# Block 1 of a gated linear attention kernel: four rows of Q times state move from VectorE to GpSimd, and the engines' calls are put in other orders

## The reference

```
state = state * f[i] + v[i] * k[j]        # 8x8 per head, scan over 1024 tokens
o[i]  = sum over j of state[i, j] * q[j]
```

## Time and profile before

| | |
|---|---|
| median of 3 runs | 510.62 us (509.84 to 511.73) |
| the profiled execution | 511.23 us |
| its span, first to last instruction | 509.4 us |
| mean granted TensorE clock | 0.998 of full speed |
| busy TensorE (products) | 495.7 us |
| busy VectorE / ScalarE / GpSimd | 447.6 / 404.9 / 311.0 us |
| moved by DMA | 87.33 MB |

### The profile page before, as it was taken

How to read it: one execution, slowest core, us unless ns; L and a number is a source line. 1 busy time by engine, 2 the same in 40 slices (tenths; PEclk the granted TensorE clock), 3 DMA queues, 4 the chain that set the end, 5 groups by cost and what they waited for, 6 DMA issues and landing times. The chain is left out here.

```text
span 509.4 us, 7961 instructions
## 1 busy us (share of the span) xinstructions
PE 495.7 (97%) x2528; PEld 383.1 (75%) x2528; DVE 447.6 (88%) x708; ACT 404.9 (79%) x839; POOL 311.0 (61%) x362
## 2 busy tenths in 40 slices
PE   9989999999999999999999999999999999999995
PEld 5667787777877777777877777777877777777895
DVE  3999999999989999999899999899999899992352
ACT  5765878787888977888897887889878788868764
POOL 0742839577592838768384775848385784929341
PEclk9999999999999999999999999999999999999999
DMA  7997999935797779768988895905875850700001
GB/s 244 250 269 181 258 257 226 234 87 150 186 264 195 221 178 239 187 164 201 248 210 214 209 257 150 244 2 145 209 181 154 218 126 18 190 1 1 23 2 65
DMA packets 21772, 87.33 MB, mean 171 GB/s; under 512 B 2528, under 2 KB 3552, under 8 KB 13792
## 3 DMA queue, kind: packets, MB, share of 16 engines
q1 hardware_dynamic: 21440, 86.46, 66.9%
q10 hardware_dynamic: 288, 0.33, 0.2%
HBM read 74.72 MB, written 12.06 MB: 170 GB/s over the span
## 5 line engine op out<-in xcount | busy, mean ns | idle before, releaser
L915 ACT ACTIVATE h<-F,cols 128x512 f32<-128x512 f32 x120 | 80.4, 688 | 11.3 <-PE F L2345 10.6
L489 POOL TENSOR_TENSOR h1lo<-h,h1hi 128x512 fp32r<-128x512 f32 x60 | 76.2, 1289 | 11.9 <-ACT h1hi L908 11.8
L489 POOL TENSOR_TENSOR h2lo<-h,h2hi 128x512 fp32r<-128x512 f32 x60 | 76.0, 1288 | 6.7 <-ACT h2hi L908 6.6
L1601 DVE TENSOR_TENSOR_SCAN KJ<-g,carry,KJ 128x512 f32<-128x512 f32 x64 | 78.2, 1262 | 0.0
L2345 PE MATMUL F<-h2hi,whi 128*128 128x512 f32 (+1 forms) x256 | 74.7, 424 | 0.2
L1601 DVE TENSOR_TENSOR_SCAN KJ<-g,KJ 128x512 f32<-128x512 f32 x64 | 74.3, 1203 | 0.7 <-POOL KJ L537 0.4
L1608 DVE TENSOR_TENSOR QJ<-QJ,KJ 128x1024 f32<-128x1024 f32 x60 | 71.2, 1213 | 0.2
L2345 PE MATMUL F<-h1hi,whi 128*128 128x512 f32 (+1 forms) x256 | 68.9, 411 | 2.4 <-DVE h L1665 2.1
L550 POOL TENSOR_TENSOR KJ<-KJ,v_sb 128x512 f32<-128x512 f32 x32 | 42.4, 1332 | 43.9 <-DMA KJ<-qk_bounce 26.9
L2345 PE MATMUL F<-h1lo,whi 128*128 128x512 f32 (+1 forms) x256 | 67.1, 401 | 0.0
L2345 PE MATMUL F<-h2lo,whi 128*128 128x512 f32 (+1 forms) x256 | 65.8, 398 | 0.4 <-POOL h2lo L489 0.3
(11 more groups left out here) (183 smaller groups left out, 934.9 us busy)
## 6 DMA issues: line engine op xcount, KB each, us to landing
KJ<-qk_bounce SPq DMA_DIRECT2D x30, 1024.0 KB, 9.9
QJ<-qk_bounce SPq DMA_DIRECT2D x30, 1024.0 KB, 10.7
qk_bounce<-qk SPq DMA_DIRECT2D x30, 256.0 KB, 4.0
x_in<-in_x SPq DMA_DIRECT2D x16, 256.0 KB, 9.1
xT<-in_xT SPq DMA_DIRECT2D x15, 256.0 KB, 4.9
out<-res SPq DMA_DIRECT2D x15, 256.0 KB, 5.8
wraw<-in_wffn SPq DMA_DIRECT2D x2, 1024.0 KB, 9.4
wraw<-in_wffn SPq DMA_DIRECT2D x2, 256.0 KB, 4.7
```

Source lines behind the costliest of these rows:

```text
L489: e.tensor_tensor(h_lo[layer][:, t, :w], h[:, t, :w], h_hi[layer][:, t, :w].bitcast(f32), ALU.subtract).then_inc(lo_done[layer], 1)
L915: e.activation(dst[:, t, :WIDTH[n]], F[t][:, :WIDTH[n]], ACT.Gelu, scale=scale[t]).then_inc(gelu_done[layer], 1)
L1601: e.tensor_tensor_scan(K, g[:, :WIDTH[n]], K, init, ALU.mult, ALU.add).then_inc(scan_done, 1)
```

## The change

1. In block 1, GpSimd multiplies rows 0 to 3 of QJ by the states, in four calls of 128x512 (the new function qs_gp). VectorE keeps rows 4 to 7 (qs(1,2), qs(1,3)). Who waits for QJ of block 1 (sum_transposed(1), the fetch of K of block 3) waits for both counts.
2. kv_gp and qs_gp take the DMA's half by the row; the counting functions are written with two tables, KV_FIRST and QS_FIRST. For kv nothing changes by it.
3. save_carry waits for the one before it.
4. The lists of calls of all five engines and the table FREED are in another order. The calls themselves are the same ones. Quoted are block 0 and 1 and the places that the prediction speaks of; several hundred further lines move by one to some places.

```diff
@@ tables and counts
+    KV_FIRST, QS_FIRST = {1: 2}, {1: 2}
+        def kv_first(n):
+            return KV_FIRST.get(n, 3)
+        def qs_first(n):
+            return QS_FIRST.get(n, 0)
+        def qs_pairs(n):
+            return sum(NPAIR - qs_first(m) for m in range(1, n))
+        def qs_gpsimd(n):
+            return sum(2 * qs_first(m) for m in range(1, n))
@@ sync, fetch
-                        e.wait_ge(qs_done, NPAIR * (n - 2))
+                        e.wait_ge(qs_done, qs_pairs(n - 1))
+                        e.wait_ge(qs_gp_done, qs_gpsimd(n - 1))
@@ gpsimd
+            def qs_gp(n, j):
+                if j % 2 == 0:
+                    e.wait_ge(Q_landed[2 * j // HD][n % 2], fetched(n))
+                e.wait_ge(scan_done, HD * n + j + 1)
+                Q = rows(QJ, n)[:, j, :]
+                e.tensor_tensor(Q, Q, rows(KJ, n)[:, j, :], ALU.mult).then_inc(qs_gp_done, 1)
@@ scalar, save_carry
+                if n:
+                    e.wait_ge(carry_done, n)
@@ vector, add
-                e.wait_ge(qs_done, NPAIR * (n - 1) + p + 2)
+                e.wait_ge(qs_done, qs_pairs(n) + p + 2)
@@ tensor, sum_transposed
-                    e.wait_ge(qs_done, NPAIR * n)
+                    e.wait_ge(qs_done, qs_pairs(n + 1))
+                    e.wait_ge(qs_gp_done, qs_gpsimd(n + 1))
@@ gpsimd, order of blocks 0 and 1
             qsj_gp(0)
             kvj_gp(2)
             kvj_gp(4)
+            qsj_gp(1)
+            qsj_gp(2)
             scale_w3()
-            qsj_gp(1)
             kvj_gp(6)
-            qsj_gp(2)
             qsj_gp(3)
             kv_gp(1, 4)
             rstd_of(0, "o")
             kv_gp(1, 5)
             kv_gp(1, 6)
             rstd_of(0, "1")
+            qs_gp(1, 0)
+            qs_gp(1, 1)
             kv_gp(1, 7)
+            qs_gp(1, 2)
+            qs_gp(1, 3)
             lo(1, 0, 0)
@@ vector, order of blocks 0 and 1
+            scan(0, 4)
             kvj(7)
-            scan(0, 4)
+            qsj(4)
             scan(0, 5)
-            qsj(4)
+            qsj(5)
             scan(0, 6)
-            qsj(5)
+            qsj(6)
             scan(0, 7)
-            qsj(6)
+            qsj(7)
             kv(1, 0)
-            qsj(7)
+            stats_o(0)
             kv(1, 1)
-            stats_o(0)
             scan(1, 0)
+            half_norm("o")
             scan(1, 1)
-            half_norm("o")
+            gated_y0()
             scan(1, 2)
-            gated_y0()
-            scan(1, 3)
             residual_1(0)
             find_low_parts()
             stats_1(0)
+            scan(1, 3)
             scan(1, 4)
+            half_norm("1")
             scan(1, 5)
             scan(1, 6)
             set_flag()
-            half_norm("1")
-            qs(1, 0)
-            qs(1, 1)
             x1_lo(0)
             scan(1, 7)
-            qs(1, 2)
             hmul(0, 0)
             hmul(0, 1)
+            qs(1, 2)
             qs(1, 3)
@@ scalar, the new order from the end of block 0's attention
+            tanh(3)
+            silu_gate(0)
+            norm_o(0)
+            silu_gate(1)
+            affine(0)
+            split_weights(1)
+            sum_low_parts(3)
+            copy_k(3)
+            center_w3()
+            norm_1(0)
+            copy_q(2)
+            split_weights(2)
+            x1_hi(0)
+            split_weights(3)
+            silu(0, 0)
+            silu(0, 1)
+            copy_v(2)
+            silu_gate(2)
@@ scalar, block 5's q (before: copy_v(5), hi(2, 2, 3), copy_q(5))
             gelu(1, 2, 3)
+            copy_q(5)
+            norm_2(1)
             hi(2, 2, 3)
@@ tensor, before the loop
-            project_gate(0)
             sum_j(6)
             sum_j(7)
+            project_f(3)
             keep_busy(4, back)
+            keep_busy(1, back)
+            project_gate(0)
             project_gate(1)
+            transpose_y(0)
             project_v(2)
-            keep_busy(1, back)
-            project_f(3)
-            transpose_y(0)
             project_k(3)
             attention_out(0)
             keep_busy(10, F[3])
-            count_low_parts()
             project_q(2)
             keep_busy(16, F[3])
             transpose_x1(0)
+            count_low_parts()
@@ tensor, start of the loop
-                project_q(3)
                 up_hi(0, 2, low_parts)
-                up_lo(0, 2, low_parts)
                 up_hi(0, 3, low_parts)
+                up_lo(0, 2, low_parts)
                 up_lo(0, 3, low_parts)
+                project_q(3)
                 sum_transposed(1)
@@ tensor, blocks 13 and 14
-                project_gate(15)
                 mid_hi(2, 13, 1, low_parts)
...
                 up_lo(14, 3, low_parts)
+                project_gate(15)
                 mid_open(1, 14, 0, low_parts)
@@ vector, blocks 14 and 15
+            kv(15, 0)
             stats_o(14)
             hmul(13, 2)
             hmul(13, 3)
-            kv(15, 0)
             kv(15, 1)
@@ sync, block 5
-            load_xT(6)
-            store(0)
+            send(5, 0)
             fetch(5, 1, 0)
             fetch(5, 1, 1)
-            send(5, 0)
```

More of the change, by code:

```diff
@@ L467, in _ @@
             fetch(15, 0, 0)
+            load_x(14)
+            store(10)
+            load_x(15)
             fetch(15, 0, 1)
@@ L1118, in _ @@
             affine(3)
+            save_carry(3)
+            copy_k(5)
+            gelu(1, 2, 1)
             hi(2, 2, 0)
-            gelu(1, 2, 1)
-            copy_k(5)
+            hi(2, 2, 1)
             gelu(1, 2, 2)
-            hi(2, 2, 1)
             hi(2, 2, 2)
             gelu(1, 2, 3)
-            copy_v(5)
+            copy_q(5)
+            norm_2(1)
             hi(2, 2, 3)
-            copy_q(5)
+            silu_gate(5)
             norm_1(3)
             gelu(2, 2, 0)
+            x1_hi(3)
             gelu(2, 2, 1)
-            x1_hi(3)
             gelu(2, 2, 2)
+            save_carry(4)
             gelu(2, 2, 3)
+            silu(3, 0)
             g_of_tanh(5)
-            silu(3, 0)
+            copy_v(5)
             silu(3, 1)
             hi(1, 3, 0)
-            silu_gate(5)
             hi(1, 3, 1)
@@ L1156, in _ @@
             hi(2, 3, 1)
+            gelu(1, 3, 3)
             hi(2, 3, 2)
-            gelu(1, 3, 3)
-            copy_q(6)
+            tanh(7)
             hi(2, 3, 3)
@@ L1221, in _ @@
             gelu(1, 5, 2)
+            hi(2, 5, 1)
+            copy_q(8)
             gelu(1, 5, 3)
-            hi(2, 5, 1)
             hi(2, 5, 2)
+            tanh(8)
             hi(2, 5, 3)
             norm_1(6)
+            copy_k(9)
+            gelu(2, 5, 0)
+            copy_v(8)
+            save_carry(7)
             x1_hi(6)
-            tanh(8)
-            gelu(2, 5, 0)
             gelu(2, 5, 1)
             gelu(2, 5, 2)
+            g_of_tanh(8)
             gelu(2, 5, 3)
@@ L2122, in _ @@
             add(14, 0)
+            x1_lo(13)
+            add(14, 1)
             qs(14, 3)
-            add(14, 1)
             add(14, 2)
             hmul(13, 0)
+            hmul(13, 1)
             residual_2(12)
-            hmul(13, 1)
+            kv(15, 0)
             stats_o(14)
@@ L2943, in rest @@
                 up_lo(11, 2, low_parts)
+                project_k(14)
+                sum_transposed(12)
                 up_hi(11, 3, low_parts)
@@ L2955, in rest @@
                 mid_hi(1, 11, 3, low_parts)
-                project_q(14)
+                transpose_y(12)
+                project_k(15)
                 mid_lo(1, 11, 0, low_parts)
-                transpose_y(12)
                 mid_lo(1, 11, 1, low_parts)
@@ L2969, in rest @@
                 mid_hi(2, 11, 2, low_parts)
-                project_k(15)
+                project_v(14)
                 mid_hi(2, 11, 3, low_parts)
```

971 lines of the change are left out of this document (476 added, 495 removed).

## The result

The changed kernel takes 512.57 us (median of 12 runs, 511.5 to 513.84), the kernel before 510.45 (12 runs on the same chip, 509.76 to 511.94): a ratio of 1.0039, interval 1.0027 to 1.0051, so 2.0 us slower. Forecast was 509.9, that is 0.7 us faster. The difference is clear of the noise and has the other sign. That 512.57 still lies in the stated range, and under the 0.5% that counted as the same, is no merit of the sum: the range was drawn wide enough for rivals B, C and D. The profiled execution of after took 512.38 us (span 510.6), close to its median; that of before (511.23) lay 0.8 above its own, so the two profiles differ by 1.2 us only.

The account below looks back on a forecast made before the run. TensorE was taken as the bound, with VectorE having slack in the middle. Front -0.3, last full blocks -0.4 and other reordering 0 gave -0.7, so the median of 510.62 us would become 509.9; range 507.5 to 512.8.

Parts of the forecast that it names:

- B: Block 5: K's fetches issued behind Q's send, so TensorE waits 1.9 us for h1lo; 511.8, or 513.4; chance 0.14.
- C: Front: half_norm on VectorE waits for a GpSimd product (pair lock), middle 0.9 us lost, 510.8; chance 0.13.
- D: No place named: some of several hundred moved calls wait in an in-order queue; 512 to 514; chance 0.10.
- Parts 2 to 4: Front, block 0: stats_o(0) starts at 26.3, attention_out(0) 0.6 us earlier, half_norm at 38.95, 1.7 us earlier.
- Part 1: Block 1: two VectorE products, 2.34 us, become four on GpSimd, 5.1 us, hidden in its room at no cost.
- The paragraph on the lock: Front: VectorE and GpSimd exclude each other for some SBUF instructions; half_norm would wait by the rule; not in the sum.
- Parts 5 and 6: Main loop's start: x1_hi(0) at 41.6 against 42.70, block 1's transposes at 48.75 against 49.07; -0.3 us.
- the sum's term for the front: Up to block 1's transposes: TensorE does the same work from 0.3 us earlier; -0.3 us, bounds 0 and -1.1.
- Part 7: Last full blocks: kv(15,0) moves ahead, project_gate(15) fills TensorE's hole before mid_open(1,14); -0.4 us, bounds 0 and -1.1.
- Part 8: Middle of the kernel: all other reordering of calls, 0 us, bounds -1.5 and +1.5.
- TensorE's idle time as a whole: From 60 to 480 us: growth by over 1.5 us would be the sign of D.
- A: Whole kernel: VectorE is the bound all along, so its 2.34 us come through whole; 507.9; chance 0.13.

Follow-up runs that it names:

- experiment 12: Four kernels in one batch against the kernel before: after_again, no_lock_third, gate_changed_rest and its front with the earlier later orders; ratios 1.0033, 1.0018, 1.0001, 0.9994.
- flag_early: Changed kernel with the flag's count on TensorE and copy on VectorE back where the kernel before has them; 512.37 us, ratio 1.0029 to the kernel before.
- after_again: The changed kernel as it is, measured again against the kernel before; 512.88 us, ratio 1.0033.
- no_lock_third: Third run of no_lock, against the kernel before; 512.16 us, ratio 1.0018.
- rest_new: Kernel before up to block 1's middle layer, all products of Q on VectorE, then the changed kernel's orders; 511.76 us, ratio 1.0013 to the kernel before.
- no_lock: Changed kernel plus one wait keeping GpSimd's first two products behind half_norm; 512.52 us, ratio 1.0034 to the kernel before; repeated, 510.94 us, 0.9997.
- gate_changed_rest: Changed kernel with GpSimd's products held behind half_norm, flag early, ten fillers for sixteen, project_gate(2) before x1(0)'s transposes; 511.08 us, ratio 1.0001 to the kernel before.

## Why the prediction was wrong

**Parts 2 to 4 were right where it counts, at half_norm.** stats_o(0) 26.43 (forecast 26.3), attention_out(0) 32.97 (33.3), stats_1(0) 34.90 (35.25), half_norm at 38.44 (38.95). The gain of 1.7 us up to half_norm was there, even 0.5 more than forecast, which is what this execution began earlier. The close fit of stats_o(0) is luck: counted from the second projections it came 20.01 us behind in after and 20.43 in before, 0.42 earlier and not 1.06.

**Part 1 failed: "the four cost nothing".** I had looked for room on GpSimd's side (it was there: kv_gp(1,7) ended 41.55, the last two products at 44.0) and for waits on semaphores. The cost is neither: it sits inside a VectorE instruction. The paragraph on the lock named half_norm as the instruction that would wait, and then "The sum above has nothing of this", because no row of before showed it for tensor_scalar. That was rival C, at 0.13 and 0.9 us. half_norm lost 1.38 us, of which 0.8 reached the time, by the medians of experiment 12. The Trainium skill's rule (SBUF — State Buffer, "Who interferes with whom"), that tensor_scalar in a two-port mode takes the lock as well, is borne out by half_norm in every kernel here: 0.58 us with no product of GpSimd beside it, 1.92 to 1.96 with one in hand. (The row on the add, by the way, shows GpSimd's product ending 1.13 us after VectorE's add and not 1.28: 222.89 against 221.76. The lock stands in it all the same.) The absence of a row was no evidence, since in the kernel before GpSimd's products and half_norm never met; a rule that speaks of exactly the pair that the change brings together deserved more than 0.13.

**Parts 5 and 6 missed a wait behind x1_hi.** x1_hi(0) came at 41.27 (41.6), right, and so it did without the lock. But the steps from there went by x1_hi alone. The branch into the main loop also waits for the flag, and the diff moves count_low_parts behind the transposes of x1(0) and set_flag behind half_norm and two scans. In before the flag was set 2.6 us ahead of x1_hi's end and could be left out of the sum; here it comes last, and 1.16 us of register load and branch follow it (their rows are at the end). It is a moved step of which I costed neither the wait nor who is behind it: TensorE's whole list. About 0.9 us. silu(0,0) came at 45.19 (44.1), the transposes at 50.02 (48.75). So the sum's term for the front, -0.3, came out as +1.46 in the profiles: the lock that part 1 put at nothing, and this wait.

**Part 7 was right in its size, not in its picture.** From mid_open(1,12) to mid_open(1,14) TensorE took 56.43 us in before (403.19 to 459.62) and 56.15 in after (404.84 to 460.99): -0.28 for a forecast of -0.4. The hole was only handed on to mid_open(1,13). As VectorE is the bound in these blocks, filling TensorE's holes is worth little, as the part said.

**Part 8, "0" with bounds of 1.5, came out at about +0.7 to +1.1.** That is 0.4 to 0.8 for all the later orders (by time and by profiles) and 0.28 back for part 7. Inside the bounds. TensorE's named waits did not grow; the waits of after from 60 to 470 us, against the earlier trace rows:

```profile
DVE x_in L1683 <- PE back L2358: 15.5, 10, 6.8
...
PE F L2372 <- DVE h L1693: 2.9, 6, 1.4
```

So none of these waits carries it. Nor does TensorE's idle time as a whole, which I had named as a sign: of the 420 us from 60 to 480 it was 3.89 us, against 4.85. But the ends of products are modelled, and a short wait for weights can disappear in busy time. The rows of the weight loads show one, and it is rival B's.

**The rivals.** A (VectorE the bound all along) is out: its slack on attention products is 15.5 us, about as before (14.8). B came true in its cause and, at a smaller price, in its effect. K(5) was issued at 123.32 (forecast 123.7), and GpSimd got it later still than I had said. GpSimd's timeline, against the earlier trace rows, and TensorE's weight loads:

```profile
137.37 1.30 POOL L565 TENSOR_TENSOR KJ<-KJ,v_sb 128x512 f32<-128x512 f32 x1 [9.96 <-DMA KJ<-qk_bounce]
...
139.86 5.04 POOL L504 TENSOR_TENSOR h1lo<-h,h1hi 128x512 fp32r<-128x512 f32 x4
```

```profile
143.73 0.66 PEld L2372 LDWEIGHTS F<-h1lo,whi 128*128 128x128 f32 x3
144.96 0.99 PEld L2372 LDWEIGHTS F<-h1lo,whi 128*128 128x128 f32 x5 [0.58 <-POOL h1lo L504]
```

TensorE began this layer at 139.45, 1.03 us later than in before, with the next block's transposes inside it. The layer's low parts are waited for one by one, by the first four products of mid_lo, and not all four before the first. So the first three ran from 143.96, and the fourth waited for GpSimd's last low part, ready at 144.90: its weight load stood for 0.58 us, and the product began about 0.3 us later than the three before it had set the beat (144.96, not 144.66). I had priced this wait at 1.9.

It is not all that the late K(5) took. flag_early has the same order of calls from here on, and its K(5) landed in time (its product on GpSimd at 135.98). From this layer to the same layer of the next block TensorE took 31.05 us in after (139.45 to 170.50) and 30.07 in flag_early (139.59 to 169.66):

```profile
139.45 0.47 PE L2372 MATMUL F<-h1hi,whi 128*128 128x512 f32 x1
...
170.50 0.39 PE L2372 MATMUL F<-h1hi,whi 128*128 128x512 f32 x1
```

```profile
139.59 0.48 PE L2372 MATMUL F<-h1hi,whi 128*128 128x512 f32 x1
...
169.66 0.39 PE L2372 MATMUL F<-h1hi,whi 128*128 128x512 f32 x1
```

Most of the difference of 1.0 us builds up in three steps, each behind GpSimd: 0.2 at the transposes of QJ (139.97), 0.35 at that low part, 0.3 at the transposes of o_norm (148.20). So I put it down to the late K(5). Four of the nine profiles with the changed orders have that wait (after, after_again, no_lock_third, rest_new: 30.45 to 31.27 us for this stretch), the other five do not (30.06 to 30.08), and none of the eight with the orders of before has it. Over the nine that is a mean of 0.4 us, half of the 0.8 that the later orders cost in the profiles. It also explains a part of the spread: no_lock's three profiled executions took 511.23, 511.47 and 512.62 us, and only the last has the late K(5). Why it lands late in some executions and not in others is open. In the four, its second half landed 12.8 to 13.6 us after that fetch was issued, in the five 11.5 to 11.9, and the send of Q ahead of it took 3.1 to 3.6 us to land, against 2.0 in four of the five and 3.6 in the fifth. This fits what I had said of the send's 256 KB, and no run separates it.

C is what happened in the front, and its price, 0.9, was about right for the lock; the flag's 0.9 came on top. D named 512 to 514 without a place; the time landed there, but there were places.

With both repaired (gate_changed_rest) the change's ratio is 1.0001, 0.05 us, where my sum without them had said -0.7. What is left of the difference I put down to part 8, which no run separates there; and the repair itself brings project_gate(2) forward, which the change does not.

## What to carry to other kernels

Moving a product from VectorE to GpSimd moves it onto a lock that VectorE's own two-input SBUF instructions and its f32 tensor_scalar from SBUF need. Before doing so, list which VectorE instructions will run beside it, and price each at what is left of GpSimd's instruction; put GpSimd's work beside scans with a PSUM input and products from PSUM. When call orders change, follow every input of the first instruction that the new order is to bring forward, the flags of branches too, and ask of each fetch that is issued later who waits for its landing. Where a kernel's runs spread, compare several profiles of the same order stretch by stretch. And a hole on an engine that is not the bound moves on when it is filled.

## What the runs showed of the hardware

**The lock by kinds of instruction.** Held up by GpSimd's 1.28 us products: VectorE's tensor_scalar of 128x128 f32 from SBUF to SBUF (two of them: 1.92 to 1.96 us in place of 0.58), the product of two SBUF tiles of 128x512 (1.41 in place of 0.69) and of 128x1024 (2.22 to 2.32 in place of 1.21). Not held up, in any of the 17 profiles, when begun beside a GpSimd product of 128x512: the scan whose gate comes from PSUM (1.25 to 1.28), and the product of h with one input from PSUM (0.72 to 0.75). The o_norm form of half_norm, which reads PSUM, took 0.70 to 0.73 beside GpSimd's products of KJ.

**Who gets the lock next.** In after, GpSimd's products kept their 1.27 us; VectorE's two tensor_scalar took 0.72 and 1.32. The first ended 0.08 after GpSimd's first product (39.16 and 39.08), the second product had begun by then, and the second tensor_scalar waited it out (40.41 and 40.32). So a row of short VectorE instructions beside a row of long ones on GpSimd can pay anew for each.

**A flag on the way to a branch.** From the end of VectorE's copy of the flag to the first product behind TensorE's branch it was 1.15 or 1.16 us in all eight profiles where the flag was last. After books it to a wait for ScalarE's split. The sequencer's own records in after, which the timeline leaves out, fill it: the load of the flag into a register, 0.49 us, and the branch, 0.09, with short gaps between the steps.

```profile
L3232 PEldq TENSOR_LOAD <-flag x1: 491/491/491, 43.0 to 43.0; - x1
```
